# Attention with one head per 32-row tile, maxima over 1024 columns and one stage per layer

## The reference

```
q, k, v = x @ Wq + bq, x @ Wk + bk, x @ Wv + bv      # per head [1024, 8]
q, k = rope(q), rope(k)
scores = einsum('bhqd,bhkd->bhqk', q, k) / sqrt(8)
attn = softmax(scores, axis=-1)
out = x_or_norm + einsum('bhqk,bhkd->bhqd', attn, v) @ Wo + bo
```

## Time and profile before

| | |
|---|---|
| median of 3 runs | 3090.01 us (3089.11 to 3093.02) |
| profiled execution | 3090.28 us, its span 3089.0 us |
| TensorE busy (matmuls) | 2512.2 us, 81% |
| TensorE busy (weight loads) | 1535.9 us, 50% |
| VectorE busy | 2231.1 us, 72% |
| ScalarE busy | 1469.7 us, 48% |
| GpSimd busy | 689.0 us, 22% |
| mean granted TensorE clock | 0.880 |
| attention of the first layer | about 784 to 1690 us |
| attention of the second layer | about 1787 to 2693 us |

### The profile page before, as it was taken

One profiled execution on the slowest core, in us unless ns is written; L12 is line 12 of the kernel. 1 busy time (PEld: TensorE's weight loads), 2 busy tenths in 40 slices (PEclk: granted clock), 3 DMA queues, 4 the chain that ended last, 5 costly groups with the idle time before them and its releaser, 6 DMA issues. The chain is left out here.

```text
span 3089.0 us, 40405 instructions
## 1 busy us (share of the span) xinstructions
PE 2512.2 (81%) x13194; PEld 1535.9 (50%) x13194; DVE 2231.1 (72%) x4681; ACT 1469.7 (48%) x2880; POOL 689.0 (22%) x602
## 2 busy tenths in 40 slices
PE   6888838823799999999998579999999999838930
PEld 5666727612455455455454335554545545428930
DVE  6766766635888788788787788878878878756635
ACT  3444312401166566666665116666666666513520
POOL 2222204665301010010100330101001010003644
PEclk9999957956699999999999769999999999957965
DMA  4000011422200000000000220000000000111211
GB/s 159 0 0 0 0 34 51 89 72 77 69 11 21 12 21 11 12 21 11 22 11 25 82 68 11 21 12 21 11 12 21 11 22 11 57 49 40 69 49 49
DMA packets 64046, 103.91 MB, mean 34 GB/s; under 512 B 12097, under 2 KB 44993, under 8 KB 63585
## 3 DMA queue, kind: packets, MB, share of 16 engines
q1 hardware_dynamic: 54880, 82.97, 8.7%
q0 software_dynamic: 8960, 18.37, 2.5%
HBM read 68.26 MB, written 33.03 MB: 33 GB/s over the span
## 5 line engine op out<-in xcount | busy, mean ns | idle before, releaser
L1080 DVE TENSOR_REDUCE mh<-psum 128x1 f32<-128x512 f32 x2048 | 1269.0, 683 | 275.1 <-PE psum L830 275.1
L1058 ACT ACTIVATE p<-psum 128x512 f32<-128x512 f32 x2048 | 1068.5, 603 | 509.3 <-PE psum L989 504.7
L830 PE MATMUL psum<-kp,qs 128*128 128x512 f32 x2176 | 903.4, 430 | 29.8 <-POOL kp L823 28.6
L989 PE MATMUL psum<-qs,kp 128*128 128x512 f32 x2048 | 855.2, 423 | 46.3 <-issue 35.1
L989 PEld LDWEIGHTS psum<-qs,kp 128*128 128x128 f32 x2048 | 386.7, 190 | 473.6 <-ACT p L1058 365.2
L830 PEld LDWEIGHTS psum<-kp,qs 128*128 128x128 f32 x2176 | 426.0, 196 | 248.1 <-DVE mh L1080 109.4
L1004 PE MATMUL psum<-p,v_ext 128*32 128x512 f32 x4096 | 543.8, 604 | 0.0
L948 POOL MEMSET qs<- 32x1024 f32 x32 | 30.3, 946 | 966.4 <-PE psum L989 966.0
L152 PE MATMUL psum<-ident,xn 128*128 128x128 f32 x160 | 44.3, 454 | 245.0 <-DVE xn L120 200.5
L514 POOL DMA_INDIRECT x_in<-n_rows,token_of x152 | 166.5, 1095 | 250.3 <-POOLq L73 183.3
L570 ACT ACTIVATE hid<-psum,stage 128x128 f32<-128x128 f32 x448 | 132.5, 367 | 180.2 <-PE psum L540 180.2
(11 more groups left out here) (178 smaller groups left out, 2386.9 us busy)
## 6 DMA issues: line engine op xcount, KB each, us to landing
qs<-qk_parts SPq DMA_DIRECT2D x114, 128.0 KB, 2.8
kf<-qk_parts SPq DMA_DIRECT2D x114, 128.0 KB, 2.9
answers<-y_out SPq DMA_DIRECT2D x152, 64.0 KB, 1.5
ew<-in_moe SPq DMA_DIRECT2D x1, 5136.0 KB, 19.5
ew<-in_moe SPq DMA_DIRECT2D x1, 4624.0 KB, 14.2
n_rows<-xn SPq DMA_DIRECT2D x8, 512.0 KB, 3.2
qk_parts<-qh SPq DMA_DIRECT2D x8, 512.0 KB, 2.7
qk_parts<-ql SPq DMA_DIRECT2D x8, 512.0 KB, 2.6
```

Source lines behind the costliest of these rows:

```text
L830: return pe.matmul(bank, a["qs"][:, g, i * P:(i + 1) * P], a["kp"][:, g, j, h * HALF:(h + 1) * HALF], start=True, stop=True)
L989: pe.matmul(psum[:, S_BANK + n % NS, :], a["kp"][:, g, j, i * P:(i + 1) * P], a["qs"][:, g, h * HALF:(h + 1) * HALF], start=True, stop=Tru ...
L1058: act.activation(a["p"][:, n % NP, h * HALF:(h + 1) * HALF], psum[:, S_BANK + (NH * n + h) % NS, :], ACT.Exp, scale=DH ** -0.5).then_inc(e ...
L1080: dve.tensor_reduce(a["mh"][:, u, h:h + 1], bank, AX.X, ALU.max).then_inc(used, 1)
```

## The change

A head's three terms and one row for the maximum are 25 rows (`ROWS_QK`). Each head of a group now has a 32-row tile of its own (partitions 32j to 32j+31, the rest zero), in the queries (`qs`) and the keys (`ks`). No masked copies are made. Score and maximum matmuls read 32 partitions, and neighbours in the program order are on different tiles where the order allows it (`heads`, `units`). Values stay in place for all sequences in `v_ext` (9 columns a head), and a weighing takes 32 of its columns from where its head begins, so that columns past the ninth belong to the following heads and their outputs are not used.

A maximum is now taken over 1024 columns, two banks at once, written straight to `mx`; the ring for fills has two places of two banks. The turned maxima are copied to `m_row`, and four DMAs per group put them into row 24 of each head's tile; the keys' row holds -1. One stage per layer runs all 16 groups as 256 steps of 4 scores (one bank of output columns, all key tiles of a half before the next half), with the maxima 40 tiles ahead (`LEAD`), 8 of these followed by a matmul whose result is not used (`WARM`). A step's weighing stands between the third and the fourth score of the step after. Outputs are turned and projected among the steps. The core of the diff:

```diff
+VE = DH + 1
+ROWS_QK = 3 * DH + 1
+PART_STORES = 6
+KT = 32
+KM = KT // GR
...
-NKF = 2
-NP = 8
+NKF = 4
+NP = 3 * GH
 S_BANK, NS = 0, 3
-M_BANK, NM = 3, 3
-O_BANK = 6
-MAX_UNITS = 30
+M_BANK, NM = 3, 2
+O_BANK = 7
+STEPS = NH * NT
+LEAD = 40
+WARM = 8
+GROUPS = B * NG
+def fill_plan():
+    plan = [[] for _ in range(GROUPS * STEPS + 8)]
+    first = [("max", *divmod(u, UN)) for u in range(LEAD)]
+    first.insert(UN, ("turn_max", 0, 0))
+    for u in range(LEAD, GROUPS * UN):
+        s = (u - LEAD) // 2
+        plan[s].append(("max", *divmod(u, UN)))
+    for g in range(GROUPS):
+        if g:
+            plan[STEPS * g - 3].append(("turn_max", g, 0))
+        for h in range(NH):
+            plan[STEPS * g + NT * (h + 1) + 1].append(("turn_out", g, h))
+        if g % NG == NG - 1:
+            s = STEPS * (g + 1)
+            plan[s + 3] += [("turn_o", g // NG, h) for h in range(NH)]
+            plan[s + 5] += [("project", g // NG, h) for h in range(NH)]
+    return first, plan
...
+    heads = ((2, 0), (3, 1))
+    units = [j for _ in range(NT) for step in range(2) for j in heads[step]]
...
+            def load(g):
+                if g >= NKF:
+                    sp.wait_ge(scored, GH * STEPS * (g - NKF + 1))
...
+            def store_maxima(g):
+                sp.wait_ge(turned, g + 1)
+                for j in range(GH):
+                    r = GR * j + ROWS_QK - 1
+                    sp.dma_start(a["qs"][r:r + 1, g % NKF, :].bitcast(F32).rearrange("r (i c) -> r i c", c=P),
+                                 a["m_row"][NT * j:NT * (j + 1), g % 2, :].bitcast(F32)).then_inc(row[g % 2], 16)
...
+                    for h in parts:
+                        r = slice(j // KM * KT, (j // KM + 1) * KT)
+                        last = pe.matmul(psum[:, bank + h, :], a["qs"][r, g % NKF, i * P:(i + 1) * P],
+                                         a["ks"][r, g % NKF, j % KM, h * HALF:(h + 1) * HALF], start=True, stop=True)
...
+            def score(s, j):
+                g, (h, i) = s // STEPS, divmod(s % STEPS, NT)
+                n = GH * s + j
+                if s % STEPS == 0 and j == 0:
+                    pe.wait_ge(row[g % 2], 16 * GH * (g // 2 + 1))
+                if n >= NS:
+                    pe.wait_ge(exped, n - NS + 1)
...
+            def weigh(s):
+                pe.wait_ge(exped, GH * (s + 1))
...
+            for n, f in enumerate(first):
+                fill(f)
+                if n >= len(first) - WARM:
+                    pe.matmul(psum[:, S_BANK, 0:HALF // 2], w.att[layer][5], t["y_t"][:, 0:HALF // 2], start=True, stop=True)
+            for s in range(nsteps):
...
+                score(s, 0)
+                if one:
+                    fill(one, (0,))
+                score(s, 1)
+                if one:
+                    fill(one, (1,))
+                score(s, 2)
+                if s:
+                    weigh(s - 1)
+                if two:
+                    fill(two, (0,))
+                score(s, 3)
+                if two:
+                    fill(two, (1,))
+                for f in todo:
+                    fill(f)
...
+                    dve.tensor_reduce(a["mx"][:, g % 2, c:c + 1], psum[:, bank:bank + 2, :].rearrange("p a d -> p (a d)"),
+                                      AX.X, ALU.max).then_inc(used, 1)
...
+            if b == B - 1:
+                pool.memset(a["qs"][:, :, :].bitcast(F32), 0.0)
+                pool.memset(a["ks"][:, :, :, :].bitcast(F32), 0.0)
```

More of the change, by code:

```diff
@@ L711, in attention_inputs @@
             (block, *sems, proj_done, rot_used, summed, high, low, v_done, rot_a, copied, mixed):
-        stored, before = t["parts_stored"], b * 64 + (1 + 64 * B * layer)
+        stored, before = t["parts_stored"], PART_STORES * 16 * (B * layer + b)
         @block.sync
         def _(sp):
[L716 to L720, removed]
+            for k, (first, second, third) in enumerate((("qh", "qh", "ql"), ("kh", "kl", "kh"))):
+                for i, part in enumerate((first, second, third)):
+                    sp.wait_ge(low if part in ("ql", "kl") else high, NH * (k + 1))
+                    sp.dma_start(t["parts"][b, k, :, i * DH:(i + 1) * DH, :],
+                                 a[part][:, :].bitcast(F32)).then_inc(stored, 16)
         @block.tensor
@@ L820, in mask_group @@
[L820 to L837, removed]
@@ new lines, in attention, with place @@
+def attention(nc, t, w, layer, a):
+    psum = t["psum"]
+    first, plan = fill_plan()
+    fills = first + [f for at in plan for f in at]
+    number = {f: n for n, f in enumerate(fills)}
+    by_act = [f[0] == "turn_o" for f in fills]
+    nsteps = GROUPS * STEPS
+    heads = ((2, 0), (3, 1))
+    units = [j for _ in range(NT) for step in range(2) for j in heads[step]]
+    def place(u):
+        return u // GH, units[u]
+    with stage(nc, "loaded0", "loaded1", "loaded2", "loaded3", "row0", "row1", "filled", "used", "turned",
+               "scored", "exped", "weighed", "out_copied", "recip", "o_copied") as \
+            (block, loaded0, loaded1, loaded2, loaded3, row0, row1, filled, used, turned,
+             scored, exped, weighed, out_copied, recip, o_copied):
+        loaded, row = (loaded0, loaded1, loaded2, loaded3), (row0, row1)
@@ L867, in _ @@
[L867 to L876, removed]
-                score_for_maximum(pe, a, psum[:, M_BANK + n % NM, :], 0, u, h).then_inc(filled, 1)
-            pe.wait_ge(merged, 1)
-            pe.transpose(psum[0:UN, M_BANK, 0:P], a["mx"][:, 0, :], t["ident"][:, :]).then_inc(turned, 1)
@@ L953, in _ @@
+            for g in range(GROUPS):
+                store_maxima(g)
+                if g + 3 < GROUPS:
+                    load(g + 3)
         @block.tensor
@@ L1039, in _ @@
+            weigh(nsteps - 1)
+            for at in plan[nsteps:]:
+                for f in at:
+                    fill(f)
         @block.scalar
         def _(act):
[L1041 to L1047 removed]
```

360 lines of the change are left out of this document (140 added, 220 removed).

## The result

The changed kernel takes 3704.76 us (median of 4 runs, 3679.54 to 3708.96) against 3090.65 (4 runs): 1.197 times as long, interval 1.192 to 1.202. The forecast was 2965, so the time lies outside the range, on the side of the rival "the clock falls". The profiled execution took 3702.76 us with a span of 3701.4; its mean granted clock is 0.602, that of before was 0.880.

A forecast was written before the change was run, and what follows sets the result against it. TensorE was taken to set the old 3.04 us period. Per layer, start 56, steps 712, fills 54 + 12 and end 7 gave 841 against 905.6; two layers, less 4 for inputs, saved 125: 3090.3 to 2965, range 2830 to 3110.

The forecast's parts named there:

- the clock falls: Rival: attention steps run at half clock, a loop of 4.6 us, 3890 us if all 512 steps do; chance 0.10.
- (a): Score and maximum matmuls over 32 rows: neighbours on different row tiles overlap, between none (0.23 each) and a pair for one.
- two 0.33 in the old period: TensorE's old 3.04 us period: both 0.33 us spacings taken as steps between 128*128 and 128*32 matmuls.
- (b): Attention steps: a loop from exp to exp through the waiting score and the weighing binds, 2.78 us with overlap, 2.91 without.
- (c): Maxima over 1024 columns: reduces of 1.21 us, two per step 2.26, so VectorE is close but doesn't bind.
- The extra fills: Turned maxima and outputs taking a ring place among the steps: 1.2 us each, 45 per layer, 54 us.
- (d): Row stores by DMA, four per group: land in 5.5 to 6.8 us, before the score due at 7.3, costing nothing.
- The start: Start of a layer's attention: 7 us to the first matmul, then 40 maxima at half clock; 56 us together.
- The inputs: Input stages: later key store and constant rows, +4 us together; POOL's clearing hidden, at most 12.6 us a layer if visible.
- no overlap: Rival: row tiles don't run side by side, a step stays at 3.04 us, 3098 us in all; chance 0.18.
- a tighter loop: Rival: weights loaded ahead and an earlier fourth score make the exp loop 2.56 us, 2852 us in all; chance 0.14.

The follow-up runs named there:

- one-tile kernel: The changed kernel with all score and maximum matmuls on the first head's 32-row tile, the other three heads' scores not computed; 4364.03 us.
- 64-row kernel: The changed kernel with row tiles of 64 instead of 32 (KT = 64), two heads to a tile, the other head's keys zero; 2943.60 us.

## Why the prediction was wrong

**The step that failed** is the one by which the sum takes all steps at the full clock. The prediction named the rival and priced it, and gave it 0.10 with this argument against: "the streaming in a step (eight times 0.21 and the weighing), even overlapped, fills over two thirds of it, and the periods of now stay at 0.98". The first half is nearly so (eight times 0.21 in pairs, 0.84, and 0.99 are 0.66 of 2.78) and did not help: even a stream without waits over 32 rows ran at 0.50 (the one-tile kernel). The second half carried a row of 128-row matmuls over to 32-row ones, which no row of before showed; a bound from both sides would have given this case far more weight. What the runs put in its place: in this kernel 32-row scores and maxima stay at 1.2 GHz for all but 79 us, and 64-row and 128-row ones with the same order hold 2.4 GHz for the layer. That the rows make the difference is shown by a constant changed alone (3704.76 to 2943.60). What in them counts isn't settled: between 32 and 64 rows it is the rows that a matmul reads and also the values on them (at 64 a key column has 25 rows that aren't zero, the queries 50), and no run took the two apart. Nor is it known why an added 32-row matmul in each step gave 307 us at the full clock for 79.

**The rival's price.** "All 512 steps 3890 us" used a half-clock loop of 4.6. It is 4.07: 0.05 + 0.72 (for 0.88) + 1.87 (for 1.98) + 0.83 (1308.66 to 1309.49, for 1.1) + 0.60. With 4.07 the same sum gives 2965 + 512 x 1.29 = 3625. A group takes 70.88 us (turned maxima at 920.02 and 990.90), 5.8 more than its 16 steps, where the sum has 54 / 16 = 3.4: 32 groups x 2.4 = 77 more. The two starts add 26 and the inputs 17 (below), and the 79 us at the full clock save about 30 steps x 1.47 = 44. That is 3701, against 3702.8 for the profiled execution, closer than its terms are known.

**The rest, by its own steps,** is read from the 64-row kernel, where the clock is as assumed; its 2943.6 us stand 21 below the forecast.

- (a) Overlap of row tiles: right, and it goes beyond pairs. Starts coincide within 0.01 us (1303.56 twice; with 32 rows 1761.93 twice, and four within 0.02 us from 1308.66 on), while on one tile they stand 0.23 apart. Of the two 0.33 in the old period only the second is a step between forms, though the prediction says it of both; the first is between two 128*128 matmuls, right behind the weighing. The sum stays.
- (b) The loop through the exp binds: right, with ScalarE idle before the fourth exp of a step. Its size is 2.60 to 2.62, not 2.78: 0.05 + 0.42 + 1.00 + 0.53 + 0.60. The mis-sized term is the one from the weighing's end to the exp, 0.53 (1761.93 to 1762.46) for 0.69. The score does not come second at all: it starts with the maximum matmul. 512 x 0.17 = 87 us less.
- (c) Reduces of 1.22 us, VectorE beside TensorE's loop: right. The extra fills: a group takes 45.94 us (turned maxima at 907.04 and 952.98), 4.2 more than 16 steps, three fills at 1.4 for 1.2: 90 x 0.2, so 18 us more in two layers.
- (d) Row stores: no score waited for them. The waits of the scores are on ScalarE or the issue alone. Right.
- The start: 69 us for 56 (793.30 to 862.5). First matmul 8.8 us after the load, for 7; the fills come at 1.27 each, as forecast, but the eight that a warm-up matmul follows take 2.3 each:

```profile
802.10 1.22 PE L923 MATMUL psum<-ks,qs 32*128 32x512 f32 x4 [19.03 <-DMA ks<-qk_parts]
804.63 2.35 PE L923 MATMUL psum<-ks,qs 32*128 32x512 f32 x4 [1.31 <-DVE mx L1043]
```

- The inputs: 4 us was too little. Measured in the changed kernel 21 (from the load of the rotary tables to a group's first load 179.0 us instead of 168.0 in the first layer, 106.8 instead of 96.4 in the second). The clearing of `qs` and `ks` was not all hidden: in the second layer the last sequence's first store comes 27.2 us behind that of the sequence before instead of 22.5, 4.7 more. While GpSimd clears `ks` there (3.54 us from 2082.68), a VectorE instruction on 128x8 (L119, from 2083.68) takes 2.56 us and ends with the clearing; in the sequence before (2059.00) it takes 0.17. The stores take 0.52 us to issue instead of 0.33 and land after 4.5 us instead of 2.6; that this comes from more and shorter pieces is not shown.
- Sum at the full clock: for each layer 69 + 256 x 2.61 + 45 x 1.4 + 19 = 819, and 818.9 was measured in the 64-row kernel's first layer, against 841 forecast. With 27 us instead of 4 outside the layers there (first load at 798.5, and 110.0 us between the layers) 2965 - 87 + 18 + 26 + 23 = 2945, for 2943.6.

The other rivals: "no overlap" did not happen, as the same starts show; "a tighter loop", at 2.56, is nearer the 2.61 of the steps at full clock than the forecast's 2.78, and came about by half, through its second term alone (0.53 for 0.59, the first being 0.42 and not 0.33).

## What to carry to other kernels

Packing small matmuls on row tiles gives the overlap and can cost the clock for it, which is worth far more: look at the granted clock of the steps, not at how much of a window TensorE's records cover. Where a matmul needs 32 rows, run the version over 64 with zeros beside it as well; here it kept all of the overlap that mattered and was 761 us faster. When a change alters the shape of what TensorE streams, a clock seen with the old shape is no evidence for the new one, and its loss belongs in the range.

## What the runs showed of the hardware

- At 32 rows the clock was 0.50 with TensorE's records over 199.2 of 200 us and no wait between matmuls; at 64 and 128 rows it was 1.0 with 193.7 and 190.6 of 200.
- The full clock, once risen over 32-row steps, was lost after some 24 to 27 us, whether row tiles overlapped (the changed kernel) or not (one tile); with one more 32-row matmul a step it held for up to 75.1 us. Each of these stretches of 24 and 27 us began within 1.5 us of the last of 16 matmuls over 128 rows.
- Matmuls over 32 rows on four row tiles, with outputs over all 128 columns, started within 0.02 us of each other (1308.66 on), and a matmul whose tile was taken started after later ones on free tiles (1309.25 against 1308.67).
- A change between 128 and 32 rows costs 0.29 us at 1.2 GHz (0.72 for 0.43 us), each way.
- While GpSimd cleared `ks`, a VectorE instruction on 128x8 took 2.56 us instead of the 0.17 of the sequence before (2083.68 and 2059.00 in the changed kernel).
- Warm-up matmuls among paced 32-row fills did not raise the clock (0.50 from 793 to 862) and cost 1 us each (2.30 for 1.27 a fill).
